# Scaling the other LoRA factor, and LoRA products by pairs of batches, in a fused two-layer conditional residual kernel

## The chip, the cores and the metric

One core of a Trainium2 chip. The metric is the device time of one execution in microseconds, lower is better. Median of three runs of the kernel before: 57.18 us (57.12 to 57.25).

## The reference

The input x is 8 batches x 512 tokens x 256 channels in float32, cond is 8 x 8. Two conditional linear layers follow each other, each with a residual:

```
w_bot = einsum('bg,got->bot', cond, weight * mask)            # weight 8 x 256 x 256
x = x + einsum('bnt,bot->bno', x, w_bot) + bias0
lora  = einsum('bter,eor,be->bto', einsum('btc,erc->bter', x, As), Bs, cond)   # As 8 x 16 x 256, Bs 8 x 256 x 16
x = x + einsum('btc,oc->bto', x, W_base) + b_base + 2 * lora
```

The 8 experts and 16 ranks of the second layer are together 128, one partition each.

## The kernel before

The kernel never computes the middle x. For each batch b it builds W0[b] = I + the mixed first weight, and W1[b] = I + base + LoRA, multiplies them to one 256 x 256 matrix M[b] (a merge), and applies M[b] to the tokens (an apply). Every matmul operand of merge, apply and LoRA is split into a high part, rounded to the reduced float32 format of TensorE, and a low part, the rest; `product` (lines 118 to 131) issues hi x hi, hi x lo and lo x hi, so each product is three matmuls per 128-row piece. In `product`, `mid_ready` is a wait before the second kind and `lo_ready` one before the third.

All engines run programs written out by hand in a fixed order and meet at semaphores.

- PE: 28 warm-up matmuls, lora(0), lora(1), then `mixed(0)` to `mixed(7)` (the first layer's weights, 128 columns each) with lora(2) and lora(3) among them; the first halves of merge 0 and 1; lora(4); the second halves of merge 0 and 1; apply(0); the two bias matmuls (line 547); then for b = 1 to 7: merge(b+1), apply(b), lora(b+4), as long as these exist (lines 550 to 555). A merge is 12 matmuls of 256 columns, an apply 12 of 512, a LoRA product 6 of 256: for each half j, A (scaled by batch b's condition) is the loaded operand and B the streamed one.
- ACT rounds the high parts: first eight `a_hi` (A_er times the condition of batch b), then W1_hi, W0_hi, x_hi, M_hi, and writes the output half 0 (`out0`), which adds bias_sb.
- DVE makes the low parts `a_lo`, x_lo and M_lo, adds base to each LoRA product (`w1`, line 323), masks the mixed weights (`w0`), does three dot products for the bias (line 362), puts bias_sb together (line 417) and writes the output half 1 (`out1`, line 357). Its loop at lines 422 to 427 runs out1(b-1), w1(b+3), x_lo(b+1), M_lo(b+1).
- POOL adds the identities and makes W0_lo and W1_lo.
- SP issues the loads and then the stores. ACT's queue issues the load of B (line 267) and of base.

PSUM has eight banks: ps_out0 to 3 (also used by mixed), ps_merge0 and 1, ps_lora0 and 1. LoRA product b goes to ps_lora[b % 2], both halves in one bank of 512 columns. The bias sums lie in ps_lora1; for that reason lora(4)'s w1 must be early, `pe.wait_ge(w1_done, 4)` stands before the bias matmuls, and lora(5) waits for bias_done. W1 has four buffers.

Of the kernel before, what the change touches and what calls it, by code (L numbers as in the profile page):

```python
# [5 lines left out]
def conditional_residual_kernel(nc: bass.Bass, head: bass.AP, rest: bass.AP, packs: bass.AP, factors_A: bass.AP,  # L6
# [22 lines left out]
    EXPW = KQ * C  # L29
    PACKW = EXPW + NT * TQ  # L30
    SCALING = 32.0 / 16
    LEAD = 4
    XBUF = 4
    W1BUF = 4
    WARM = 28
# [5 lines left out]
    with ExitStack() as ctx:  # L41
        def sb(name, shape, dt=f32):
            return ctx.enter_context(nc.sbuf_tensor(name, shape, dt))
# [4 lines left out]
        def sem(name):  # L48
            return ctx.enter_context(nc.semaphore(name))
# [28 lines left out]
        bias_sum = sb("bias_sum", [P, NT])  # L78
        base_bias0 = sb("base_bias0", [P, NT])
        low_bias = sb("low_bias", [P, NB])  # L80
        bias_sb = sb("bias_sb", [P, NT, NB])
        B_hi = sb("B_hi", [P, C], f32r)
        B_lo = sb("B_lo", [P, C], f32r)
        A_hi = sb("A_hi", [P, NB, C], f32r)
        A_lo = sb("A_lo", [P, NB, C], f32r)
# [18 lines left out]
        ps_out = [pb(f"ps_out{i}", [P, TOK]) for i in range(2 * NT)]  # L104
# [2 lines left out]
        ps_mix = ps_out  # L107
        ps_last = ps_lora[0][:, 0, :]

        ps_bias = ps_lora[1][:, 0, 0:NT * NB].rearrange("p (j b) -> p j b", j=NT)  # L110

# [5 lines left out]

        warm_set, ident_zero, ident_done = sem("warm_set"), sem("ident_zero"), sem("ident_done")  # L120
        base_done, dots_done, low_done, fixed_done = sem("base_done"), sem("dots_done"), sem("low_done"), sem("fixed_done")
        bias_mm, bias_done, bhi_done, blo_done = sem("bias_mm"), sem("bias_done"), sem("bhi_done"), sem("blo_done")

        ahi_done, alo_done = sem("ahi_done"), sem("alo_done")
        lora_mm, w1_done, w1hi_done, w1lo_done = sem("lora_mm"), sem("w1_done"), sem("w1hi_done"), sem("w1lo_done")
# [97 lines left out]

        @block.scalar
        def _(act):
            def a_hi(b):
                nc.scalar.activation(A_hi[:, b], A_er, ACT.Copy,
                                     scale=cond_er[:, b:b + 1]).then_inc(ahi_done, 1)

            def w1_hi(b):  # L230
                act.wait_ge(w1_done, b + 1)

                if b >= W1BUF:
                    act.wait_ge(merge_mm, b - W1BUF + 1)
                nc.scalar.activation(W1_hi[:, b % W1BUF], W1[:, b % W1BUF], ACT.Copy).then_inc(w1hi_done, 1)  # L235
# [34 lines left out]
            nc.scalar.activation(table_sb[:, :], warm[:, 0:1], ACT.Copy)  # L270
            act.dma_start(base_sb[:, :, :], base.rearrange("p (j o) -> p j o", j=NT)).then_inc(base_in, 16)

            act.wait_ge(lora_arrived, 16)
            for b in range(NB):
                a_hi(b)
            w1_hi(0)
            w1_hi(1)

# [23 lines left out]
            b = NB - 1  # L302
# [6 lines left out]
        def _(dve):  # L309
            nc.vector.memset(warm[:, :], 0.0).then_inc(warm_set, 1)  # L310

            def a_lo(b):
                dve.wait_ge(ahi_done, b + 1)
                nc.vector.scalar_tensor_tensor(out=A_lo[:, b], in0=A_er, scalar=cond_er[:, b:b + 1],
                                               in1=A_hi[:, b].bitcast(f32),
                                               op0=ALU.mult, op1=ALU.subtract).then_inc(alo_done, 1)

            def w1(b):
                dve.wait_ge(lora_mm, b + 1)
                if b >= W1BUF:  # L320

                    dve.wait_ge(w1lo_done, b - W1BUF + 1)
                nc.vector.tensor_tensor(W1[:, b % W1BUF], ps_lora[b % 2][:, :, :], base_sb[:, :, :],  # L323
                                        ALU.add).then_inc(w1_done, 1)

            def w0(q):
                dve.wait_ge(mix_mm, q + 1)
# [37 lines left out]
            def ramp_low(b):  # L365
                dve.wait_ge(ramp_hi, b + 2)
                nc.vector.tensor_tensor(W0_lo[:, b, :, H:C], W0[:, b, :, H:C], W0_hi[:, b, :, H:C].bitcast(f32),
                                        ALU.subtract).then_inc(ramp_lo, 1)

            dve.wait_ge(B_arrived, 16)  # L370
            nc.vector.tensor_scalar(B_hi[:, :], B_er, SCALING, None, ALU.mult).then_inc(bhi_done, 1)
            dve.wait_ge(bhi_done, 1)
            nc.vector.scalar_tensor_tensor(out=B_lo[:, :], in0=B_er, scalar=SCALING, in1=B_hi[:, :].bitcast(f32),
                                           op0=ALU.mult, op1=ALU.subtract).then_inc(blo_done, 1)
            dve.wait_ge(lora_arrived, 16)
            for b in range(NB):
                a_lo(b)
            nc.vector.tensor_tensor(bias_sum[:, :], bias0, bias1, ALU.add).then_inc(fixed_done, 1)
            dve.wait_ge(fixed_done, 1)
            w0(0)  # L380
# [26 lines left out]
            m_lo(1)  # L407
            split_x_lo(1)

            for j in range(NT):  # L410
                dve.wait_ge(dots_done, 1 + j)
                dot(base_rows[:, j, :], base_bias0[:, j:j + 1]).then_inc(dots_done, 1)
            dve.wait_ge(dots_done, 1 + NT)

            dve.wait_ge(bias_mm, 1)
            for j in range(NT):
                last = nc.vector.tensor_scalar(bias_sb[:, j, :], ps_bias[:, j, :], base_bias0[:, j:j + 1],
                                               bias_sum[:, j:j + 1], ALU.add, ALU.add)
            last.then_inc(bias_done, 1)
            dve.wait_ge(bias_done, 1)  # L420
            for b in range(1, NB):
                out1(b - 1)
                if b + 3 < NB:
                    w1(b + 3)
                if b + 1 < NB:
                    split_x_lo(b + 1)
                    m_lo(b + 1)
# [8 lines left out]
        def _(pe):  # L436
            def product(out, terms, lo_ready=None, mid_ready=None):


                for n, (hi_l, _, hi_r, _) in enumerate(terms):  # L440
                    nc.tensor.matmul(out, hi_l, hi_r, start=(n == 0), stop=False)  # L441
                if mid_ready is not None:
                    pe.wait_ge(*mid_ready)
                for hi_l, _, _, lo_r in terms:
                    nc.tensor.matmul(out, hi_l, lo_r, start=False, stop=False)  # L445
                if lo_ready is not None:
                    pe.wait_ge(*lo_ready)
                for n, (_, lo_l, hi_r, _) in enumerate(terms):
                    mm = nc.tensor.matmul(out, lo_l, hi_r, start=False, stop=(n == len(terms) - 1))  # L449
                return mm  # L450

            def lora(b):

                pe.wait_ge(ahi_done, b + 1)
                if b == 0:
                    pe.wait_ge(bhi_done, 1)
                if b >= 2:
                    pe.wait_ge(w1_done, b - 1)
                if b == 5:
                    pe.wait_ge(bias_done, 1)  # L460
                for j in range(NT):
                    cols = slice(j * P, (j + 1) * P)
                    mm = product(ps_lora[b % 2][:, j, :],
                                 [(A_hi[:, b, cols], A_lo[:, b, cols], B_hi[:, :], B_lo[:, :])],
                                 lo_ready=(alo_done, b + 1),
                                 mid_ready=(blo_done, 1) if b == 0 and j == 0 else None)
                mm.then_inc(lora_mm, 1)

            def mixed(q):
# [63 lines left out]
            for b in range(2):  # L533
                pe.wait_ge(ramp_hi, 1)
                pe.wait_ge(w1lo_done, b + 1)
                merge_half(b, 0, (ramp_first, 1))
            lora(4)
            for b in range(2):
                pe.wait_ge(ramp_hi, 2 + b)
                merge_half(b, 1, (ramp_lo, 1 + b)).then_inc(merge_mm, 1)  # L540

            pe.wait_ge(w0_done, NQ)
            apply(0)
            pe.wait_ge(w1_done, 4)
# [5 lines left out]
            for b in range(1, NB):  # L550
                if b + 1 < NB:
                    merge(b + 1)
                apply(b)
                if b + LEAD < NB:
                    lora(b + LEAD)


# [52 lines left out]
```

## Time and profile before

| | |
|---|---|
| median of 3 runs | 57.18 us (57.12 to 57.25) |
| profiled execution, its own time | 57.23 us |
| its span in the trace | 55.4 us, 997 instructions |
| PE busy | 51.7 us, 93% of the span |
| DVE busy | 42.1 us, 76% |
| ACT busy | 31.5 us, 57% |
| POOL busy | 31.2 us, 56% |
| DMA | 11.79 MB, mean 213 GB/s |

Times are microseconds from the start of the span. PE is the matmul stream; matmuls are pipelined, so the distance from one start to the next is the pace, and the printed duration of a matmul is longer than that. The duration of a row with x2 or more is from the first start to the last end of the group. The number in brackets is the idle time of the engine before the row and what ended it. 1.8 us lie outside the span and inside the measured time.

### The profile page before, as it was taken

The numbers are of one execution on the slowest core, as the hardware profiler recorded it, in microseconds if no ns is written. First come the engines' busy times: TensorE is split into PE (matmuls) and PEld (weight loads), VectorE is DVE, ScalarE is ACT, GpSimd is POOL, SyncE is SP. The second block draws the span as 40 slices with busy tenths as digits, with TensorE's granted clock in tenths as the row PEclk, the third lists the DMA queues.
The fourth block names the chain that finished last, engine by engine and source line by source line (L and its number), as shares of the span: only waits on it lengthen the run. The fifth ranks groups of instructions, "written<-read, shape, count | busy, mean of one in ns | idle before, by whom it ended". The sixth has DMA issues, their size and how long they took to land.

```text
span 55.4 us, 997 instructions
## 1 busy us (share of the span) xinstructions
PE 51.7 (93%) x342; PEld 47.1 (85%) x342; DVE 42.1 (76%) x64; ACT 31.5 (57%) x52; POOL 31.2 (56%) x30
## 2 busy tenths in 40 slices
PE   2999999999999999999999999999999999999900
PEld 2988999999999888988998898899889889888800
DVE  0039999979596998999999999979929959805030
ACT  1949900447807889440999925970993950840800
POOL 4003400299980099999909999999966990000000
PEclk9999999999999999999999999999999999999999
DMA  0699999999999994000082540090054045049572
GB/s 0 133 392 335 373 366 389 419 418 425 408 396 417 417 393 169 9 0 0 0 306 78 222 169 0 15 364 0 6 195 183 0 185 194 0 179 382 197 284 95
DMA packets 5476, 11.79 MB, mean 213 GB/s; under 512 B 608, under 2 KB 1376, under 8 KB 5472
## 3 DMA queue, kind: packets, MB, share of 16 engines
q1 hardware_dynamic: 5184, 11.35, 54.6%
q10 hardware_dynamic: 288, 0.39, 1.9%
q8 instruction: 2, 0.03, 0.3%
q14 instruction: 2, 0.02, 0.1%
HBM read 7.54 MB, written 4.19 MB: 212 GB/s over the span
## 4 chain that ended last, share of the span: by engine, by line
PE 93%; DVE 1%; issue 0%
PE ps_out L441 13%; PE ps_out L483 13%; PE ps_out L445 13%; PE ps_out L449 13%; PE ps_merge L441 7%; PE ps_merge L445 7%; PE ps_merge L449 7%; PE ps_merge L522 6%; PE ps_lora L441 5%; PE ps_lora L445 5%; PE ps_lora L449 5%; DVE out_sb L432 1%; PE ps_lora L547 1%; DVE warm L310 0%
## 5 line engine op out<-in xcount | busy, mean ns | idle before, releaser
L189 POOL TENSOR_TENSOR W_lo<-W,W_hi 128x512 fp32r<-128x512 f32 x8 | 10.5, 1314 | 7.1 <-ACT W_hi L235 7.1
L342 DVE TENSOR_TENSOR x_lo<-x_sb,x_hi 128x1024 fp32r<-128x1024 f32 x8 | 12.7, 1584 | 0.0
L195 POOL TENSOR_TENSOR W_lo<-W,W_hi 128x512 fp32r<-128x512 f32 x6 | 10.9, 1824 | 0.0
L441 PE MATMUL ps_out<-x_hi,M_hi 128*128 128x512 f32 (+1 forms) x32 | 9.8, 388 | 0.0
L445 PE MATMUL ps_out<-x_lo,M_hi 128*128 128x512 f32 (+1 forms) x32 | 9.7, 384 | 0.0
L449 PE MATMUL ps_out<-x_hi,M_lo 128*128 128x512 f32 (+1 forms) x32 | 9.7, 384 | 0.0
L248 ACT ACTIVATE M_hi<-ps_merge 128x512 fp32r<-128x512 f32 x8 | 4.8, 597 | 8.0 <-PE ps_merge L449 8.0
L255 ACT ACTIVATE x_hi<-x_sb 128x1024 fp32r<-128x1024 f32 x8 | 8.4, 1053 | 0.0
L199 POOL TENSOR_TENSOR W<-W,ident 128x256 f32<-128x256 f32 x6 | 6.6, 1099 | 3.0 <-DVE x_lo L342 3.0
L357 DVE TENSOR_SCALAR out_sb<-ps_out,bias_sb 128x512 f32<-128x512 f32 x7 | 5.2, 747 | 3.5 <-PE ps_out L449 3.4
L264 ACT ACTIVATE out_sb<-ps_out,bias_sb 128x512 f32<-128x512 f32 x8 | 5.5, 685 | 3.9 <-PE ps_out L449 2.2
L483 PE MATMUL ps_out<-packs_sb 128*128 128x128 f32 x64 | 7.6, 275 | 0.0
L483 PEld LDWEIGHTS ps_out<-packs_sb 128*128 128x128 f32 x64 | 7.4, 192 | 0.0
L235 ACT ACTIVATE W_hi<-W 128x512 fp32r<-128x512 f32 x8 | 5.0, 626 | 3.9 <-DVE W L323 3.8
L449 PEld LDWEIGHTS ps_out<-x_hi,M_lo 128*128 128x128 f32 x32 | 5.9, 188 | 1.2
L445 PEld LDWEIGHTS ps_out<-x_lo,M_hi 128*128 128x128 f32 x32 | 5.9, 188 | 1.2
L441 PE MATMUL ps_merge<-W_hi 128*128 128x256 f32 x32 | 6.7, 291 | 0.0
L445 PE MATMUL ps_merge<-W_lo,W_hi 128*128 128x256 f32 x32 | 6.4, 283 | 0.0
L449 PE MATMUL ps_merge<-W_hi,W_lo 128*128 128x256 f32 x32 | 6.4, 282 | 0.0
L441 PEld LDWEIGHTS ps_out<-x_hi,M_hi 128*128 128x128 f32 x32 | 5.5, 189 | 0.9 <-issue 0.2
L331 DVE TENSOR_TENSOR W<-ps_out,packs_sb 128x512 f32<-128x512 f32 x8 | 5.4, 686 | 0.9 <-PE ps_out L483 0.9
L349 DVE TENSOR_TENSOR M_lo<-ps_merge,M_hi 128x512 fp32r<-128x512 f32 x8 | 5.5, 682 | 0.4 <-ACT M_hi L248 0.4
(50 smaller groups left out, 80.1 us busy)
## 6 DMA issues: line engine op xcount, KB each, us to landing
x_sb<-xT_dram SPq DMA_DIRECT2D x8, 512.0 KB, 10.2
outT_dram<-out_sb SPq DMA_DIRECT2D x15, 256.0 KB, 2.3
packs_sb<-packs_dram SPq DMA_DIRECT2D x7, 288.0 KB, 5.3
rows_sb<-rows_dram SPq DMA_DIRECT2D x1, 384.0 KB, 6.8
base_sb<-base_dram ACTq DMA_DIRECT2D x1, 256.0 KB, 3.6
outT_dram<-out_sb SPq DMA_DIRECT2D x2, 128.0 KB, 1.8
packs_sb<-head_dram SPq DMA_DIRECT2D x1, 192.0 KB, 3.4
packs_sb<-rest_dram SPq DMA_DIRECT2D x1, 160.0 KB, 3.6
```

The source lines that it names most:

```text
L189: pool.tensor_tensor(W1_lo[:, b % W1BUF], W1[:, b % W1BUF], W1_hi[:, b % W1BUF].bitcast(f32), ALU.subtract).then_inc(w1lo_done, 1)
L195: pool.tensor_tensor(W0_lo[:, b % 2], W0[:, b], W0_hi[:, b % 2].bitcast(f32), ALU.subtract).then_inc(w0lo_done, 1)
L199: pool.tensor_tensor(diagonal(b), diagonal(b), ident[:, :].unsqueeze(1).to_broadcast([P, NT, P]), ALU.add).then_inc(eye_done, 1)
L255: nc.scalar.activation(x_hi[:, b % XBUF], x_sb[:, b], ACT.Copy).then_inc(xhi_done, 1)
L264: nc.scalar.activation(out_sb[:, b % 2, 0, :], ps_out[b % 2 * NT][:, :], ACT.Identity, bias=bias_sb[:, 0, b:b + 1]).then_inc(out_done[0], 1)
L331: nc.vector.tensor_tensor(W0[:, :, :, ts].rearrange("p b j t -> p j b t"), ps_mix[q % 4][:, :].rearrange("p (j b t) -> p j b t", j=NT, t=T ...
L342: nc.vector.tensor_tensor(x_lo[:, b % XBUF], x_sb[:, b], x_hi[:, b % XBUF].bitcast(f32), ALU.subtract).then_inc(xlo_done, 1)
L349: nc.vector.tensor_tensor(M_lo[:, b % 2], ps_merge[b % 2][:, :, :], M_hi[:, b % 2].bitcast(f32), ALU.subtract).then_inc(mlo_done, 1)
L441: nc.tensor.matmul(out, hi_l, hi_r, start=(n == 0), stop=False)
L445: nc.tensor.matmul(out, hi_l, lo_r, start=False, stop=False)
L449: mm = nc.tensor.matmul(out, lo_l, hi_r, start=False, stop=(n == len(terms) - 1))
L483: mm = nc.tensor.matmul(dst[:, j, :, k, :], pack(q)[0][:, k, j * P:(j + 1) * P], mix, start=True, stop=True)
```

## The change

Three things change.

1. The condition of batch b now scales B, not A. `a_hi(b)` and `a_lo(b)` become `b_hi(b)` on ACT and `b_lo(b)` on DVE, eight each as before; the factor 2 is now on A, split once on DVE. ACT waits for both loads before its first b_hi. A is the same for all batches, so two batches can be streamed behind one loaded operand.
2. LoRA products 4 to 7 go by pairs: `lora_pair(4)` takes the place of lora(4), `lora_pair(6)` comes after apply(2), and no LoRA product follows apply(1) and apply(3). A pair is 6 matmuls of 512 columns (two batches of 256); half j goes to ps_lora[j]. DVE's `w1_pair` adds base in two operations of 512 columns, one per half, at b = 1 and b = 3 of its loop, where the single w1(4) to w1(7) ran at b = 1 to 4.
3. The bias sums move to ps_out3. DVE reads them with one operation (`low_sum`, adding bias_sum) before the two base dots, and PE waits for that read before the second half of apply(1). bias_sb is then one operation instead of two.

```diff
-        ps_bias = ps_lora[1][:, 0, 0:NT * NB].rearrange("p (j b) -> p j b", j=NT)
+        ps_bias = ps_out[3][:, 0:NT * NB].rearrange("p (j b) -> p j b", j=NT)
...
-            def a_hi(b):
-                nc.scalar.activation(A_hi[:, b], A_er, ACT.Copy,
-                                     scale=cond_er[:, b:b + 1]).then_inc(ahi_done, 1)
+            def b_hi(b):
+                nc.scalar.activation(B_hi[:, b], B_er, ACT.Copy,
+                                     scale=cond_er[:, b:b + 1]).then_inc(bhi_done, 1)
             def w1_hi(b):
-                act.wait_ge(w1_done, b + 1)
+                act.wait_ge(w1_done, b + 1 if b < SINGLE else b // 2 * 2 + 2)
...
+            act.wait_ge(B_arrived, 16)
             act.wait_ge(lora_arrived, 16)
             for b in range(NB):
-                a_hi(b)
+                b_hi(b)
...
+            def w1_pair(b):
+                dve.wait_ge(lora_mm, SINGLE + (b - SINGLE) // 2 + 1)
+                dve.wait_ge(w1lo_done, b - W1BUF + 2)
+                at = b % W1BUF
+                for j in range(NT):
+                    nc.vector.tensor_tensor(W1[:, at:at + 2, j, :], ps_lora[j][:, :, :],
+                                            base_sb[:, j, :].unsqueeze(1).to_broadcast([P, 2, C]),
+                                            ALU.add).then_inc(w1_done, 1)
...
+            dve.wait_ge(lora_arrived, 16)
+            nc.vector.tensor_scalar(A_hi[:, :], A_er, SCALING, None, ALU.mult).then_inc(ahi_done, 1)
+            dve.wait_ge(ahi_done, 1)
+            nc.vector.scalar_tensor_tensor(out=A_lo[:, :], in0=A_er, scalar=SCALING, in1=A_hi[:, :].bitcast(f32),
+                                           op0=ALU.mult, op1=ALU.subtract).then_inc(alo_done, 1)
             dve.wait_ge(B_arrived, 16)
...
+            dve.wait_ge(bias_mm, 1)
+            nc.vector.tensor_tensor(low_sum[:, :, :], ps_bias, bias_sum[:, :].unsqueeze(2).to_broadcast([P, NT, NB]),
+                                    ALU.add).then_inc(bias_read, 1)
             for j in range(NT):
                 dve.wait_ge(dots_done, 1 + j)
                 dot(base_rows[:, j, :], base_bias0[:, j:j + 1]).then_inc(dots_done, 1)
             dve.wait_ge(dots_done, 1 + NT)
-            dve.wait_ge(bias_mm, 1)
-            for j in range(NT):
-                last = nc.vector.tensor_scalar(bias_sb[:, j, :], ps_bias[:, j, :], base_bias0[:, j:j + 1],
-                                               bias_sum[:, j:j + 1], ALU.add, ALU.add)
-            last.then_inc(bias_done, 1)
+            dve.wait_ge(bias_read, 1)
+            nc.vector.tensor_tensor(bias_sb[:, :, :], low_sum[:, :, :],
+                                    base_bias0[:, :].unsqueeze(2).to_broadcast([P, NT, NB]), ALU.add).then_inc(bias_done, 1)
             dve.wait_ge(bias_done, 1)
             for b in range(1, NB):
                 out1(b - 1)
-                if b + 3 < NB:
-                    w1(b + 3)
+                if b == 1 or b == 3:
+                    w1_pair(b + 3)
...
             def lora(b):
-                if b == 5:
-                    pe.wait_ge(bias_done, 1)
...
                     mm = product(ps_lora[b % 2][:, j, :],
-                                 [(A_hi[:, b, cols], A_lo[:, b, cols], B_hi[:, :], B_lo[:, :])],
-                                 lo_ready=(alo_done, b + 1),
-                                 mid_ready=(blo_done, 1) if b == 0 and j == 0 else None)
+                                 [(A_hi[:, cols], A_lo[:, cols], B_hi[:, b], B_lo[:, b])],
+                                 lo_ready=(alo_done, 1) if b == 0 and j == 0 else None,
+                                 mid_ready=(blo_done, b + 1) if j == 0 else None)
...
+            def lora_pair(b):
+                pe.wait_ge(blo_done, b + 2)
+                pe.wait_ge(w1_done, b)
+                both = slice(b, b + 2)
+                for j in range(NT):
+                    cols = slice(j * P, (j + 1) * P)
+                    mm = product(ps_lora[j][:, :, :], [(A_hi[:, cols], A_lo[:, cols], B_hi[:, both], B_lo[:, both])])
+                mm.then_inc(lora_mm, 1)
...
+                    if b == 1 and i == 1:
+                        pe.wait_ge(bias_read, 1)
...
-            lora(4)
+            lora_pair(4)
...
-            pe.wait_ge(w1_done, 4)
             pe.wait_ge(low_done, 1)
...
                 apply(b)
-                if b + LEAD < NB:
-                    lora(b + LEAD)
+                if b == 2:
+                    lora_pair(6)
```

## Rows read from the trace of the kernel before

**Rows 1.** Chain of work that ended last, share of the span by engine.
```profile
PE 93%; DVE 1%; issue 0%
```

**Rows 2.** PE in order of time, 26 to 30 us: start, duration, engine, line, operation.
```profile
26.65 0.28 PE L441 MATMUL ps_lora<-B_hi,A_hi 128*128 128x256 f32 x1
...
27.37 0.40 PE L441 MATMUL ps_merge<-W_hi 128*128 128x256 f32 x2
...
28.81 0.63 PE L441 MATMUL ps_out<-x_hi,M_hi 128*128 128x512 f32 x2
29.27 0.62 PE L445 MATMUL ps_out<-x_lo,M_hi 128*128 128x512 f32 x2
29.74 0.62 PE L449 MATMUL ps_out<-x_hi,M_lo 128*128 128x512 f32 x2
```

**Rows 3.** All engines in order of time, 3 to 6 us.
```profile
3.50 3.30 ACT L227 ACTIVATE A_hi<-lora_sb 128x256 fp32r<-128x256 f32 x8 [0.82 <-DMA lora_sb<-factors_A_dram]
3.68 0.29 DVE L371 TENSOR_SCALAR B_hi<-lora_sb 128x256 fp32r<-128x256 f32 x1 [2.75 <-DMA lora_sb<-factors_B_dram]
...
4.35 3.66 DVE L314 SCALAR_TENSOR_TENSOR A_lo<-lora_sb,A_hi 128x256 fp32r<-128x256 f32 x8
...
4.49 0.58 PE L445 MATMUL ps_lora<-B_lo,A_hi 128*128 128x256 f32 x1
...
5.26 0.41 PE L441 MATMUL ps_lora<-B_hi,A_hi 128*128 128x256 f32 x1
...
5.47 0.41 PE L445 MATMUL ps_lora<-B_lo,A_hi 128*128 128x256 f32 x1
```

**Rows 4.** PE in order of time: behind lora(4), and the bias matmuls.
```profile
17.46 0.50 PE L441 MATMUL ps_merge<-W_hi 128*128 128x256 f32 x2
...
22.03 0.51 PE L547 MATMUL ps_lora<-low_bias,lora_sb 128*128 128x8 f32 x4
```

**Rows 5.** DVE in order of time, from 19 us on.
```profile
19.86 0.66 DVE L362 CUSTOM_DVE_ANT_0 row_products<-lora_sb,rows_sb 128x256 f32<-128x256 f32 x1
...
21.42 0.69 DVE L349 TENSOR_TENSOR M_lo<-ps_merge,M_hi 128x512 fp32r<-128x512 f32 x1 [0.27 <-ACT M_hi L248]
22.02 1.43 DVE L342 TENSOR_TENSOR x_lo<-x_sb,x_hi 128x1024 fp32r<-128x1024 f32 x1
23.38 0.97 DVE L362 CUSTOM_DVE_ANT_0 row_products<-rows_sb 128x256 f32<-128x256 f32 x1
...
24.39 1.39 DVE L362 CUSTOM_DVE_ANT_0 row_products<-rows_sb 128x256 f32<-128x256 f32 x1
...
25.82 0.48 DVE L417 TENSOR_SCALAR bias_sb<-ps_lora,base_bias,bias_sum 128x8 f32<-128x8 f32 x2
...
27.00 0.68 DVE L323 TENSOR_TENSOR W<-ps_lora,base_sb 128x512 f32<-128x512 f32 x1
27.60 1.22 DVE L342 TENSOR_TENSOR x_lo<-x_sb,x_hi 128x1024 fp32r<-128x1024 f32 x1
28.73 0.68 DVE L349 TENSOR_TENSOR M_lo<-ps_merge,M_hi 128x512 fp32r<-128x512 f32 x1
...
30.59 2.19 DVE L342 TENSOR_TENSOR x_lo<-x_sb,x_hi 128x1024 fp32r<-128x1024 f32 x1
...
41.55 0.75 DVE L357 TENSOR_SCALAR out_sb<-ps_out,bias_sb 128x512 f32<-128x512 f32 x1 [0.99 <-PE ps_out L449]
```

**Rows 6.** ACT in order of time, 18 to 21 us.
```profile
18.48 0.60 ACT L248 ACTIVATE M_hi<-ps_merge 128x512 fp32r<-128x512 f32 x1 [0.24 <-PE ps_merge L449]
...
20.27 0.63 ACT L241 ACTIVATE W_hi<-W 128x512 fp32r<-128x512 f32 x1 [0.24 <-POOL W L199]
20.80 0.58 ACT L248 ACTIVATE M_hi<-ps_merge 128x512 fp32r<-128x512 f32 x1
```

**Rows 7.** POOL in order of time, beside the dots and x_lo(3).
```profile
24.02 1.47 POOL L189 TENSOR_TENSOR W_lo<-W,W_hi 128x512 fp32r<-128x512 f32 x1
...
30.40 1.30 POOL L195 TENSOR_TENSOR W_lo<-W,W_hi 128x512 fp32r<-128x512 f32 x1
```

More of the change, by code:

```diff
@@ L31, in conditional_residual_kernel @@
     SCALING = 32.0 / 16
-    LEAD = 4
+    SINGLE = 4
     XBUF = 4
@@ L80, in conditional_residual_kernel @@
         low_bias = sb("low_bias", [P, NB])
+        low_sum = sb("low_sum", [P, NT, NB])
         bias_sb = sb("bias_sb", [P, NT, NB])
[L82 to L85, printed above, removed]
+        A_hi = sb("A_hi", [P, C], f32r)
+        A_lo = sb("A_lo", [P, C], f32r)
+        B_hi = sb("B_hi", [P, NB, C], f32r)
+        B_lo = sb("B_lo", [P, NB, C], f32r)
         W1 = sb("W1", [P, W1BUF, NT, C])
@@ L121, in conditional_residual_kernel @@
         base_done, dots_done, low_done, fixed_done = sem("base_done"), sem("dots_done"), sem("low_done"), sem("fixed_done")
-        bias_mm, bias_done, bhi_done, blo_done = sem("bias_mm"), sem("bias_done"), sem("bhi_done"), sem("blo_done")
+        bias_mm, bias_read, bias_done, bhi_done, blo_done = sem("bias_mm"), sem("bias_read"), sem("bias_done"), sem("bhi_done"), sem("blo_done")
         ahi_done, alo_done = sem("ahi_done"), sem("alo_done")
@@ L310, in _, with b_lo @@
             nc.vector.memset(warm[:, :], 0.0).then_inc(warm_set, 1)
[L312 to L316, printed above, removed]
+            def b_lo(b):
+                dve.wait_ge(bhi_done, b + 1)
+                nc.vector.scalar_tensor_tensor(out=B_lo[:, b], in0=B_er, scalar=cond_er[:, b:b + 1],
+                                               in1=B_hi[:, b].bitcast(f32),
+                                               op0=ALU.mult, op1=ALU.subtract).then_inc(blo_done, 1)
             def w1(b):
                 dve.wait_ge(lora_mm, b + 1)
-                if b >= W1BUF:
-                    dve.wait_ge(w1lo_done, b - W1BUF + 1)
-                nc.vector.tensor_tensor(W1[:, b % W1BUF], ps_lora[b % 2][:, :, :], base_sb[:, :, :],
+                nc.vector.tensor_tensor(W1[:, b], ps_lora[b % 2][:, :, :], base_sb[:, :, :],
                                         ALU.add).then_inc(w1_done, 1)
+            def w1_pair(b):
[6 more added lines that the diff above has]
+                                            ALU.add).then_inc(w1_done, 1)
             def w0(q):
@@ L368, in ramp_low @@
                                         ALU.subtract).then_inc(ramp_lo, 1)
-            dve.wait_ge(B_arrived, 16)
[L371 to L375, printed above, removed]
+            dve.wait_ge(lora_arrived, 16)
[3 more added lines that the diff above has]
+                                           op0=ALU.mult, op1=ALU.subtract).then_inc(alo_done, 1)
+            dve.wait_ge(B_arrived, 16)
             for b in range(NB):
-                a_lo(b)
+                b_lo(b)
             nc.vector.tensor_tensor(bias_sum[:, :], bias0, bias1, ALU.add).then_inc(fixed_done, 1)
@@ L452, in lora @@
             def lora(b):
-                pe.wait_ge(ahi_done, b + 1)
+                pe.wait_ge(bhi_done, b + 1)
                 if b == 0:
-                    pe.wait_ge(bhi_done, 1)
+                    pe.wait_ge(ahi_done, 1)
                 if b >= 2:
                     pe.wait_ge(w1_done, b - 1)
-                if b == 5:
-                    pe.wait_ge(bias_done, 1)
                 for j in range(NT):
```

## Prediction

> **What bounds the kernel now.** I read the shares of the chain of work that ended last first: PE has 93% of it, DVE 1%, and issue nothing [rows 1]. So nearly every microsecond of the span is a matmul behind a matmul, and an edit counts only if it changes what PE streams or makes PE wait. The order of PE's matmuls in time then gives the pace. Six LoRA matmuls of 256 columns go from 26.65 to 27.37, 0.12 us each; twelve merge matmuls of 256 columns from 27.37 to 28.81, again 0.12 each; in the apply the first four of 512 columns go from 28.81 to 29.74, 0.2325 each [rows 2]. Next I looked at the start, where PE meets its first operands [rows 3], at the one matmul pair in the middle that is longer than its kind [rows 4], and last at DVE in order of time from 19 us on. After M_lo(1) at 21.42 each of DVE's operations down to x_lo(3) at 30.59 begins as the one before it ends: x_lo(1), the bias dots, bias_sb, out1(0), w1(4), then batch 2's operands [rows 5]. It is not on the chain, but there it is the engine that is nearly late.
>
> **How nearly.** apply(2) needs x_lo(2) for its third matmul at 29.27 and M_lo(2) for its fifth at 29.74. DVE ends x_lo(2) at 27.60 + 1.22 = 28.82 and M_lo(2) at 28.73 + 0.68 = 29.41 [rows 2, 5]. With about 0.05 for the signal (the wait at 21.42 is told by ACT's M_hi(1), 20.80 + 0.58 = 21.38, rows 5 and 6) the slack is 0.40 and 0.28 us. That is what the change spends.
>
> **The change on PE.** *Columns.* The four single products of batches 4 to 7 are 24 matmuls of 256 columns, 24 x 0.12 = 2.88 us. The two pairs are 12 of 512, 12 x 0.2325 = 2.79. Gain 0.09. Below, the gain could be nothing, above 0.15. The number of columns is the same; only the fixed part per matmul is halved in count: 2 x 0.12 - 0.2325 = 0.0075 us each.
>
> The Trainium skill (TensorE: Matmul & The Clock Gate, Back-to-back issue gap) puts the warm gap at columns over 2.4 GHz plus 2.5 ns; by that the twelve saved issues are worth 0.03 us instead of 0.09. The trace's 0.12 for 256 columns is above that rule's 0.109, so the rows decide.
>
> *Where the pair stands.* lora_pair(4) takes the place of lora(4) between the first and the second halves of merges 0 and 1. It is 6 x 0.2325 = 1.40 instead of 0.72, so what comes after it is 0.68 later. The first pair of matmuls behind it shows 0.50 [rows 4] where its like shows 0.40 [27.37, rows 2]: 0.10 us in which PE waits for W0_hi. With 0.68 more cover that wait goes: gain 0.10 (0 if it isn't a wait). After apply(1) no LoRA product follows any more, 0.72 less; after apply(2) the second pair stands, 0.68 more; after apply(3) none, 0.72 less. lora_pair(4) also needs w1(3) out of its bank. On DVE w1(3) stands ahead of w0(7), and that ahead of the W0_hi for which PE waited only these 0.10 us, one product later; I cost that wait at nothing.
>
> *Start.* ACT now waits for B besides A. A's wake is ACT's 3.50, B's is DVE's 3.68 [rows 3], so b_hi(0) starts 0.2 later, about 3.70. The first b_lo follows it as a_lo follows at 4.35 at the earliest: b_hi(0) ends near 4.20, b_lo(0) runs 4.24 to 4.72. DVE's two A operations take the place of its two B operations and start 0.18 earlier, so they are out of the way. PE's second matmul, now waiting for b_lo(0), goes from 4.49 to about 4.77; but its third no longer waits for a_lo(0), since A_lo is long done. So the fourth, at 5.26 before, comes at 4.77 + 0.16 for a load that wasn't ahead + 2 x 0.21 (pace 5.26 to 5.47, which is 256 columns at 1.2 GHz) = 5.35. Cost 0.09, of which about half is at the half clock and so is regained when the clock rises at the same moment: I take 0.08, with 0 and 0.20 as ends. After that ACT and DVE run ahead of PE as before. No DMA is added, taken away or moved on any queue.
>
> **The bias move.** The two bias matmuls keep their number and place. On DVE low_sum is added right behind x_lo(1), and the two bias_sb operations (0.48 for two, rows 5) become one: +0.24 and -0.24. low_sum waits for bias_mm: PE's bias matmuls go from 22.03 [rows 4] to 22.7 and are done near 23.2, DVE is there at 23.8; hidden. PE's new wait for bias_read stands before apply(1)'s second half, at about 25.9 when low_sum is done by 24.1; hidden by 1.8 us, and if it weren't, merge(3) and apply(2) would queue behind it. Between nothing and 0.3 on DVE; I take 0.
>
> **The DVE side, which sets the sum.** (1) M_hi(0) on ACT starts at 18.48 + 0.68 + 0.08 - 0.10 = 19.14. From it to M_hi(1) ACT took 20.80 - 18.48 = 2.32, with 0.24 of idle that a later start absorbs [rows 6], so 2.0 to 2.1: M_hi(1) at 21.19, done 21.77. M_lo(1) moves from 21.42 to 21.80, +0.37, and with it everything DVE does without a gap behind it. (2) w1_pair(4) is two operations where w1(4) was one; from 27.00 to 27.60 [rows 5] one costs 0.60. The second stands before x_lo(2): +0.60. Together 0.97: x_lo(2) ends at 29.79, M_lo(2) at 30.38. In exchange w1(5) is gone one round later, which is too late to help. On ACT W1_hi(4) now waits for both halves of the pair, from 28.6; behind it are M_hi(3) and out0(1), which nothing on PE needs before apply(3).
>
> PE wants M_lo(2) at 29.74 + 0.68 + 0.08 - 0.10 - 0.72 = 29.68, since LoRA(5) no longer stands between apply(1) and merge(3). It gets it at 30.38 + 0.05 = 30.43: a stall of 0.75, in two parts, since x_lo(2) is already late by 29.84 - 29.21 = 0.63 at the third matmul. They don't add; the later one sets it. The removed LoRA(5) was, without being meant so, part of DVE's cover.
>
> **After that.** lora_pair(6) stands behind apply(2), 1.40 us of PE work that needs no DVE operation in time, so DVE catches up: with out1(1) before it, x_lo(3) ends at latest at 31.1 + 2.19 = 33.3, while apply(3) reaches it at 30.43 + 8 x 0.2325 + 1.40 + 1.44 + 0.47 = 35.6. Before apply(4) DVE has w1_pair(6), +0.60 again, but from there on it waits for PE (0.99 idle at 41.55, rows 5). I cost it at nothing; if that cover were gone it would be at most 0.60. The end, ps_last and the stores aren't touched.
>
> **Sum.** -0.09 - 0.10 + 0.08 + 0.75 = +0.64. The profiled execution took 57.23, the median is 57.18, 0.05 lower: 57.82, so about 57.8. The likeliest case's own range is 57.5 to 58.1.
>
> **Rivals.** *A, no stall, from the dots (faster or same).* DVE's two base dots take 0.97 and 1.39 us from 23.38 and 24.39, the bias dot of the same form 0.66 [rows 5]. The second meets POOL's w1_lo(3), 24.02 to 25.49 [rows 7]. If the later start lets both dots pass when POOL is idle, DVE regains up to 0.31 + 0.73 = 1.04 us, more than the 0.97 it lost. The mechanism decides at 0.75 regained; then what is left is -0.11 (-0.24 with the better ends of columns and start): 56.95 to 57.1. Against it: POOL's work is paced by the same ACT and is busy almost throughout this stretch, so it moves with the dots.
>
> *B, more collision (slower yet).* x_lo(2) takes 1.22 because POOL is idle then; x_lo(3), started at 30.59 within POOL's operation at 30.40, takes 2.19 [rows 5, 7]. Later by a microsecond, x_lo(2) or a dot may land in one: +0.3 to +1.0, 58.1 to 58.8. For it: low_sum shifts the dots against POOL. Against: POOL's w1_lo(4) waits for ACT's W1_hi(4), which itself waits for w1_pair(4).
>
> The Trainium skill (GPSIMD Engine Reference, Specifications) says that GpSimd's SBUF interfaces are shared with VectorE and that an operation with two SBUF inputs contends. The 1.22 against 2.19 agrees.
>
> *C, the start.* The longer gap before the second matmul could also keep the clock at 1.2 GHz for longer; each microsecond of it costs half. The pace is still 0.21 at 5.47 and 0.12 in the middle [rows 2, 3]; with 1 us more of it, +0.5: 58.3.
>
> *D, the change doesn't gain columns at all:* +0.09 on the forecast, inside its range.
>
> **Chances.** Forecast (with D) 0.60; A 0.20, of which 0.13 faster and 0.07 within 0.2%; B 0.13; C 0.07. About 0.2% (0.11 us) is what a measurement here tells from no change. Faster 0.13, same 0.07, slower 0.80. The range leaves out most of faster A and the far end of B: 57.1 to 58.4.
>
> **What would show it.** After: PE idle of 0.6 to 0.9 before the third and fifth matmul of apply(2), put down to DVE x_lo and M_lo; DVE without idle from 21.8 to there; the pair behind lora_pair(4) at 0.40 instead of 0.50; 512-column LoRA matmuls 0.23 apart; first mixed matmul 0.05 to 0.10 later. It is wrong if apply(2) runs without a gap (A), if the base dots or x_lo(2) change their durations by over 0.3 (A or B), or if the pace of 0.21 lasts longer than in the kernel before (C).

## The result: slower by 2.8%, where 1.1% was forecast

| | before | changed |
|---|---|---|
| median of 6 runs | 57.3 us (57.12 to 57.63) | 59.7 us (58.94 to 61.01) |
| ratio | | 1.0284, 95% interval 1.0235 to 1.0334 |
| profiled execution, its own time | 57.23 us | 58.97 us |
| its span | 55.4 us | 57.2 us |
| PE busy | 51.7 us | 51.3 us |
| DVE busy | 42.1 us | 44.4 us |

The ratio compares undisturbed runs; three of the six of the changed kernel, at 60.4 to 61.0, were disturbed and only raise its median. The difference to explain is that of the two profiled executions: 58.97 - 57.23 = +1.74 us. The forecast was 57.8, range 57.1 to 58.4. The sign and the place were right, the size was not.

The chain of work that ended last, changed kernel, shares of the span. Before it was PE with 93% [rows 1]:

```profile
PE 66%; DVE 19%; DMA 5%; issue 4%; ACT 1%; DVEq 0%
```

PE in order of time, changed kernel: start, duration, engine, line, operation, idle before and what ended it. `product`'s three kinds are L449, L453, L457 here:

```profile
16.65 0.40 PE L449 MATMUL ps_lora<-B_hi,A_hi 128*128 128x512 f32 x1
...
18.04 0.40 PE L449 MATMUL ps_merge<-W_hi 128*128 128x256 f32 x2
...
22.47 0.60 PE L564 MATMUL ps_out<-low_bias,lora_sb 128*128 128x8 f32 x4
22.93 0.48 PE L449 MATMUL ps_merge<-W_hi 128*128 128x256 f32 x2
...
28.62 0.67 PE L449 MATMUL ps_out<-x_hi,M_hi 128*128 128x512 f32 x2
30.83 0.73 PE L453 MATMUL ps_out<-x_lo,M_hi 128*128 128x512 f32 x2 [1.54 <-DVE x_lo L350]
31.43 0.73 PE L457 MATMUL ps_out<-x_hi,M_lo 128*128 128x512 f32 x2
32.00 0.63 PE L449 MATMUL ps_out<-x_hi,M_hi 128*128 128x512 f32 x2
```

apply(2) begins at 28.62, 0.19 us earlier than before [28.81, rows 2]. At the pace of before its fifth matmul would stand at 28.62 + 0.93 = 29.55. It stands at 31.43: a stall of 1.88 us. The next pair follows 0.57 later instead of 0.46, so the stop costs 1.99 in all. The rest, -0.25, is the gain at other places. The first pair of matmuls behind lora_pair(4) shows 0.40, not 0.50 [rows 4]; lora_pair(4) took 18.04 - 16.65 = 1.39. From the first bias matmul to the merge behind it are 22.93 - 22.47 = 0.46 us, 0.36 before (22.03 to 22.39): low_bias ended only at 22.41, and where it is early (the experiment with the first dot moved) the distance is 0.36 again.

DVE in order of time, changed kernel, the lines that answer to [rows 5]. `row_products` is a dot, L370 with `lora_sb` the first one, with `rows_sb` alone the two base dots:

```profile
20.19 0.92 DVE L370 CUSTOM_DVE_ANT_0 row_products<-lora_sb,rows_sb 128x256 f32<-128x256 f32 x1
...
21.16 1.25 DVE L412 TENSOR_SCALAR low_bias<-lora_sb,A_bias 128x8 f32<-128x8 f32 x1
22.33 0.68 DVE L357 TENSOR_TENSOR M_lo<-ps_merge,M_hi 128x512 fp32r<-128x512 f32 x1
22.93 1.23 DVE L350 TENSOR_TENSOR x_lo<-x_sb,x_hi 128x1024 fp32r<-128x1024 f32 x1
24.08 0.16 DVE L419 TENSOR_TENSOR low_sum<-ps_out,bias_sum 128x16 f32<-128x16 f32 x1
24.17 1.43 DVE L370 CUSTOM_DVE_ANT_0 row_products<-rows_sb 128x256 f32<-128x256 f32 x1
...
25.64 1.39 DVE L370 CUSTOM_DVE_ANT_0 row_products<-rows_sb 128x256 f32<-128x256 f32 x1
...
27.07 0.59 DVE L426 TENSOR_TENSOR bias_sb<-low_sum,base_bias 128x16 f32<-128x16 f32 x1
27.70 0.75 DVE L365 TENSOR_SCALAR out_sb<-ps_out,bias_sb 128x512 f32<-128x512 f32 x1
28.36 1.28 DVE L330 TENSOR_TENSOR W<-ps_lora,base_sb 128x512 f32<-128x512 f32 x2
29.56 1.22 DVE L350 TENSOR_TENSOR x_lo<-x_sb,x_hi 128x1024 fp32r<-128x1024 f32 x1
30.69 0.68 DVE L357 TENSOR_TENSOR M_lo<-ps_merge,M_hi 128x512 fp32r<-128x512 f32 x1
```

POOL and ACT beside them, changed kernel:

```profile
19.39 1.44 POOL L200 TENSOR_TENSOR W<-W,ident 128x256 f32<-128x256 f32 x2 [2.93 <-DVE x_lo L350]
...
20.92 0.59 ACT L249 ACTIVATE M_hi<-ps_merge 128x512 fp32r<-128x512 f32 x1
21.10 1.29 POOL L196 TENSOR_TENSOR W_lo<-W,W_hi 128x512 fp32r<-128x512 f32 x1 [0.26 <-ACT W_hi L242]
...
23.04 2.27 POOL L190 TENSOR_TENSOR W_lo<-W,W_hi 128x512 fp32r<-128x512 f32 x1
25.28 1.47 POOL L196 TENSOR_TENSOR W_lo<-W,W_hi 128x512 fp32r<-128x512 f32 x1
26.71 0.92 POOL L200 TENSOR_TENSOR W<-W,ident 128x256 f32<-128x256 f32 x1
```

POOL and low_bias in the kernel before:

```profile
19.49 1.63 POOL L199 TENSOR_TENSOR W<-W,ident 128x256 f32<-128x256 f32 x2 [3.02 <-DVE x_lo L342]
20.56 0.59 DVE L404 TENSOR_SCALAR low_bias<-lora_sb,A_bias 128x8 f32<-128x8 f32 x1
```

x_lo(2) starts at 29.56 instead of 27.60: DVE is 1.96 us later, where 0.97 was forecast. Read the two engines side by side. low_bias works on 8 columns and takes 1.25 us, from 21.16 to 22.41, because POOL's W0_lo(2) runs from 21.10 to 22.39. Its 0.59 before was a wait too, only a shorter one: it ended at 21.15, POOL's second identity add at 21.12. The first dot came up during POOL's first identity add before (the first of the x2, over at 20.23), and in the changed kernel, 0.33 later, during the second (over at 20.83); both times it ended 0.28 behind that add. ACT's M_hi(1) stands at 20.92, only 0.12 later than before [rows 6], so it isn't ACT that holds M_lo(1) back, it is DVE's own row of operations.

The slip, step by step: M_lo(1) starts 22.33 - 21.42 = 0.91 later (0.37 forecast); from there to bias_sb it is 4.74 instead of 4.40, +0.34; from bias_sb to out1(0) and on to x_lo(2), with the second half of w1_pair, 2.49 instead of 1.78, +0.71. Sum 1.96.

### The profile page after: what moved, and what is told of

It is laid out like the page before. It is cut to its first block, busy times and chain, and to the rows that moved or that the text cites. A ratio compares the mean times of both kernels' runs of the same rounds, so it can differ in the third digit from the quotient of the medians.

```text
span 57.2 us, 969 instructions
## 1 busy us (share of the span) xinstructions
PE 51.3 (90%) x330; PEld 45.4 (80%) x330; DVE 44.4 (78%) x64; ACT 31.3 (55%) x52; POOL 31.2 (55%) x30
## 4 chain that ended last, share of the span: by engine, by line
PE 66%; DVE 19%; DMA 5%; issue 4%; ACT 1%; DVEq 0%
PE ps_out L499 12%; PE ps_out L453 10%; PE ps_out L457 9%; PE ps_out L449 8%; DMA lora_sb<-factors_A_dram 5%; PE ps_merge L457 5%; PE ps_merge L453 5%; PE ps_merge L449 5%; PE ps_lora L453 4%; DVE x_lo L350 4%; PE ps_lora L449 4%; DVE row_products L370 4%; PE ps_lora L457 4%; DVE M_lo L357 2%; DVE W L330 2%
## 5 line engine op out<-in xcount | busy, mean ns | idle before, releaser
L350 DVE TENSOR_TENSOR x_lo<-x_sb,x_hi 128x1024 fp32r<-128x1024 f32 x8 | 13.4, 1676 | 0.0
L453 PE MATMUL ps_out<-x_lo,M_hi 128*128 128x512 f32 (+1 forms) x32 | 9.8, 387 | 1.5 <-DVE x_lo L350 1.5
L449 PE MATMUL ps_out<-x_hi,M_hi 128*128 128x512 f32 (+1 forms) x32 | 9.9, 389 | 0.0
L457 PE MATMUL ps_out<-x_hi,M_lo 128*128 128x512 f32 (+1 forms) x32 | 9.8, 387 | 0.0
L453 PEld LDWEIGHTS ps_out<-x_lo,M_hi 128*128 128x128 f32 x32 | 5.9, 188 | 3.1 <-DVE x_lo L350 2.0
L457 PEld LDWEIGHTS ps_out<-x_hi,M_lo 128*128 128x128 f32 x32 | 5.9, 188 | 1.5 <-DVE M_lo L357 0.3
L449 PE MATMUL ps_merge<-W_hi 128*128 128x256 f32 x32 | 6.6, 287 | 0.0
L457 PE MATMUL ps_merge<-W_hi,W_lo 128*128 128x256 f32 x32 | 6.4, 283 | 0.0
L453 PE MATMUL ps_merge<-W_lo,W_hi 128*128 128x256 f32 x32 | 6.4, 283 | 0.0
L449 PEld LDWEIGHTS ps_out<-x_hi,M_hi 128*128 128x128 f32 x32 | 5.5, 189 | 0.9 <-issue 0.2
```

Of the source, the lines that this page charges most:

```text
L350: nc.vector.tensor_tensor(x_lo[:, b % XBUF], x_sb[:, b], x_hi[:, b % XBUF].bitcast(f32), ALU.subtract).then_inc(xlo_done, 1)
```

## The experiments

Ratios are to the kernel before, with their 95% interval. The changed kernel stands at 1.0284 and 58.97 us. Edits are shown against the changed kernel. Theory 1: the loss is DVE being late for apply(2), through the pair's place. Its rivals: the start (2), the bias move (3), the 512 columns themselves (4). Theory 5, formed on the first results: DVE's operations with SBUF operands wait for POOL's running operation, and this doubles the slip.

One distance is free of an early or late start and of the stores at the end: from the first merge matmul to the last group of matmuls, both read in order of time. It is 52.27 - 15.23 = 37.04 us before and 54.01 - 15.13 = 38.88 in the changed kernel. Below it is called the stream.

### The first part of the change alone

```diff
-            lora_pair(4)
+            lora(4)
...
-                if b == 1 or b == 3:
-                    w1_pair(b + 3)
+                if b + 3 < NB:
+                    w1(b + 3)
```

Bias sums and their code are those of before as well.

> The kernel before with only the first part of the change: the condition scales B; LoRA products all single, bias sums in the LoRA bank as before. Theory 1 (the loss comes from DVE being late for apply(2), by the pair's work and by collisions with POOL that the pair's delay brings): no change, 57.1 to 57.4, ratio 0.997 to 1.003, and no gap in apply(2). Rival 2 (the start costs): 57.5 or more with the first mixed matmul later than 6.74.

Measured: 57.42 median, fastest 57.12, ratio 1.0015 (0.9975 to 1.0055). Scaling B instead of A costs nothing that can be measured, and by the interval at most 0.3 us. The profiled execution itself, 57.80 us, has its first mixed matmul at 7.03, 0.29 later than before, which alone would look like rival 2. But with the same scaling it stands at 6.28 in the changed kernel and at 6.19 two experiments below, and the stream here is 37.02. The start differs from one execution to the next; rival 2 is out as the cause of 2.8%.

### The scaling and the bias move, products single

The same two edits for the pairs, and the bias sums as in the changed kernel.

> The scaling of B and the move of the bias sums, LoRA products all single. Theory 1: within 0.2 of the kernel before, 57.1 to 57.5; low_bias near 0.6 us, since M_lo(0) isn't delayed. Rival 3 (the bias move, with low_sum and its waits, makes the loss): 58 or more, and PE waits in apply(1) or apply(2).

Measured: 58.11 median, fastest 57.74, ratio 1.0152 (1.0098 to 1.0206). I had this wrong: with the bias move the kernel is 1.5% slower, and the scaling alone showed none of it. DVE in this kernel:

```profile
20.54 0.58 DVE L414 TENSOR_SCALAR low_bias<-lora_sb,A_bias 128x8 f32<-128x8 f32 x1
...
25.78 1.14 DVE L428 TENSOR_TENSOR bias_sb<-low_sum,base_bias 128x16 f32<-128x16 f32 x1
...
28.22 1.22 DVE L352 TENSOR_TENSOR x_lo<-x_sb,x_hi 128x1024 fp32r<-128x1024 f32 x1
```

and POOL:

```profile
25.42 1.47 POOL L196 TENSOR_TENSOR W_lo<-W,W_hi 128x512 fp32r<-128x512 f32 x1
```

bias_sb adds 16 columns from SBUF to SBUF and takes 1.14 us. It ends at 26.92, POOL's W0_lo(3) at 26.89. The two operations it replaces read PSUM and took 0.48 together [rows 5]. x_lo(2) starts 0.62 later than before, and PE waits for it in apply(2). The stream is 37.55, so this stop is 0.51 of the loss; the profiled executions differ by 58.00 - 57.23 = 0.77, and the other 0.26 lies outside the stream and stays open. The next experiment asks whether it is bias_sb, or low_sum and PE's wait for it.

### The same with bias_sb made by ACT

```diff
...
-            nc.vector.tensor_tensor(bias_sb[:, :, :], low_sum[:, :, :],
-                                    base_bias0[:, :].unsqueeze(2).to_broadcast([P, NT, NB]), ALU.add).then_inc(bias_done, 1)
...
+                    for j in range(NT):
+                        act.wait_ge(dots_done, 2 + j)
+                        nc.scalar.activation(bias_sb[:, j, :], low_sum[:, j, :], ACT.Identity,
+                                             bias=base_bias0[:, j:j + 1]).then_inc(bias_done, 1)
```

> The scaling of B and the bias move with single products, and bias_sb made by ACT (two small operations from low_sum) instead of DVE's one operation of 1.14 us. Theory 5 (an operation of DVE that reads two SBUF operands waits until POOL's running operation is over, here W0_lo(3), and that alone made the bias move cost 0.5 us or more): x_lo(2) starts at 27.6 instead of 28.22, no gap in apply(2), 57.1 to 57.4, ratio below 1.005. Rival (low_sum, the bank or PE's wait for it cost it): stays at 57.8 to 58.1.

Measured: 57.52 median, fastest 57.13, ratio 0.9996 (0.9957 to 1.0035). The whole 1.5% is gone. DVE:

```profile
26.00 0.75 DVE L372 TENSOR_SCALAR out_sb<-ps_out,bias_sb 128x512 f32<-128x512 f32 x1 [0.43 <-DVE base_bias L377]
...
27.27 1.23 DVE L357 TENSOR_TENSOR x_lo<-x_sb,x_hi 128x1024 fp32r<-128x1024 f32 x1
```

The forecast said 27.6, it is 27.27 (0.17 of the difference to 28.22 is an earlier start), apply(2) has no gap, and the stream is 37.02. The bank, low_sum (0.16, reads PSUM) and PE's wait are still there; only the operation that met POOL isn't.

### Products of 256 columns at the pairs' place

```diff
-                    mm = product(ps_lora[j][:, :, :], [(A_hi[:, cols], A_lo[:, cols], B_hi[:, both], B_lo[:, both])])
+                    for k in range(2):
+                        mm = product(ps_lora[j][:, k, :], [(A_hi[:, cols], A_lo[:, cols], B_hi[:, b + k], B_lo[:, b + k])])
```

> The changed kernel with each product of 512 columns as two of 256, at the same place and in the same banks. Theory 1: the place makes the loss and 512 columns are worth only 0.07 us for each pair, so 59.0 to 59.2 against 58.97 for the changed kernel, still a gap of 1.7 to 2.0 in apply(2). Rival 4 (512-column products are themselves slow, or hold a bank longer): 57.3 to 58.

Measured: 60.38 median, fastest 60.19, ratio 1.0572 (1.0516 to 1.0628). The trace has the stall where it was, the time is 1.2 us above what I expected:

```profile
28.88 0.66 PE L449 MATMUL ps_out<-x_hi,M_hi 128*128 128x512 f32 x2
31.07 0.73 PE L453 MATMUL ps_out<-x_lo,M_hi 128*128 128x512 f32 x2 [1.53 <-DVE x_lo L350]
```

From 28.88 to 31.07 are 2.19 us, 2.21 in the changed kernel; rival 4 is out. The stream is 39.02, 0.14 more than in the changed kernel: about what the 512 columns are worth. At the end ACT's last whole output waits for an earlier store:

```profile
54.41 0.69 ACT L265 ACTIVATE out_sb<-ps_out,bias_sb 128x512 f32<-128x512 f32 x1 [3.11 <-DMA outT_dram<-out_sb]
```

The changed kernel has 2.03 of idle time there, put down to PE. So by this one profile about 1 us of its time is a late store. Why all six of its runs are above 60 stays open, since one profile shows one store.

### w1_pair(4) after x_lo(2) and M_lo(2)

```diff
-                if b == 1 or b == 3:
+                if b == 3:
                     w1_pair(b + 3)
                 if b + 1 < NB:
                     split_x_lo(b + 1)
                     m_lo(b + 1)
+                if b == 1:
+                    w1_pair(b + 3)
```

> The changed kernel with one move: on DVE w1_pair(4) comes after x_lo(2) and M_lo(2) instead of before them. Theory 1: both are 1.2 us earlier, the stall in apply(2) falls from 1.88 to 0.7, the time to 57.8; up to 58.4 if merge(4) then waits for W1_lo(4), which follows w1_pair(4) over ACT and POOL. Rival (DVE's late start into x_lo(2) isn't what ends the wait): 58.9 as before.

Measured: 59.58 median, fastest 59.51, ratio 1.042 (1.038 to 1.0461), slower than the changed kernel. PE:

```profile
28.89 0.65 PE L451 MATMUL ps_out<-x_hi,M_hi 128*128 128x512 f32 x2
29.89 0.74 PE L455 MATMUL ps_out<-x_lo,M_hi 128*128 128x512 f32 x2 [0.34 <-DVE x_lo L350]
30.49 0.73 PE L459 MATMUL ps_out<-x_hi,M_lo 128*128 128x512 f32 x2
...
34.67 0.48 PE L451 MATMUL ps_merge<-W_hi 128*128 128x256 f32 x2 [0.71 <-issue]
...
35.87 0.50 PE L459 MATMUL ps_merge<-W_hi,W_lo 128*128 128x256 f32 x2 [0.49 <-POOL W_lo L196]
```

The stall in apply(2) is 30.49 - 28.89 - 0.93 = 0.67, as expected. But merge(4) then waits twice, 0.71 and 0.49 of idle PE. Read from start to start it is more: from the last LoRA matmul, 33.57, to apply(3), 36.92, are 3.35 us, and 36.17 - 34.51 = 1.66 in the changed kernel, so merge(4) loses 1.69 where apply(2) had won 1.21. The stream is 39.52. POOL shows why:

```profile
32.37 2.19 POOL L190 TENSOR_TENSOR W_lo<-W,W_hi 128x512 fp32r<-128x512 f32 x1 [4.49 <-ACT W_hi L236]
34.52 1.30 POOL L196 TENSOR_TENSOR W_lo<-W,W_hi 128x512 fp32r<-128x512 f32 x1
```

W1_lo(4) meets x_lo(3) on DVE (32.20 to 33.41) and takes 2.19 instead of 1.3, and W0_lo(4) comes behind it. My bound for this, 58.4, left that collision out. The wait moved from one place to the next.

### The first dot into a time when POOL is idle

```diff
+            dve.wait_ge(rows_in, 16)
+            dot(A_er, A_bias0[:, :]).then_inc(dots_done, 1)
             ramp_low(0)
...
-            dve.wait_ge(rows_in, 16)
-            dot(A_er, A_bias0[:, :]).then_inc(dots_done, 1)
```

> The changed kernel with the first bias dot (A times bias0) moved ahead of W0_lo's second halves on DVE, into a gap of 0.48 us, to a time when POOL is idle. Theory 5: the dot takes 0.66 instead of 0.92, low_bias comes sooner, M_lo(1) starts at 21.55 instead of 22.33, DVE is 0.5 to 0.8 us earlier at x_lo(2), the stall in apply(2) falls from 1.88 to 1.1 to 1.4, time 58.2 to 58.5. Rival (the dots' place doesn't matter, they are absorbed later): 58.95.

Measured: 58.29 median, fastest 58.17, ratio 1.0182 (1.0122 to 1.0241), 0.7 us less than the changed kernel. DVE:

```profile
16.78 0.42 DVE L370 CUSTOM_DVE_ANT_0 row_products<-lora_sb,rows_sb 128x256 f32<-128x256 f32 x1
...
20.19 0.66 DVE L412 TENSOR_SCALAR low_bias<-lora_sb,A_bias 128x8 f32<-128x8 f32 x1
21.53 0.69 DVE L357 TENSOR_TENSOR M_lo<-ps_merge,M_hi 128x512 fp32r<-128x512 f32 x1 [0.68 <-ACT M_hi L249]
```

The dot takes 0.42 with POOL idle, 0.66 before, 0.92 in the changed kernel. low_bias takes 0.66 instead of 1.25; it still waits for POOL, whose second identity add ends at 20.82, low_bias at 20.85. M_lo(1) is back to waiting for ACT, at 21.53 as expected, and the stall in apply(2) is 1.30. Of the 0.80 us that M_lo(1) gained x_lo(2) keeps 0.70: the first base dot is down to 0.88 from 1.43, but bias_sb, earlier now, meets another POOL operation and takes 1.14 instead of 0.59.

### Without the base dots

The two dots and their share of the bias are left out; bias_sb stays, with bias_sum in the place of what the dots gave.

> The changed kernel without the two base dots (the term base times bias0 is left out of the bias): DVE has 2.9 us less to do before x_lo(2). Theory 1: no stall in apply(2) at all, 57.0 to 57.2, which is the changed kernel's 58.97 less the stall of 1.88; so everything but the stall is a small gain against the kernel before. Rival 3 (start or pairs cost by themselves): 57.5 or more.

Measured: 56.95 median, fastest 56.84, ratio 0.9946 (0.9908 to 0.9983). apply(2) runs through:

```profile
28.55 0.63 PE L445 MATMUL ps_out<-x_hi,M_hi 128*128 128x512 f32 x2
29.02 0.62 PE L449 MATMUL ps_out<-x_lo,M_hi 128*128 128x512 f32 x2
29.48 0.62 PE L453 MATMUL ps_out<-x_hi,M_lo 128*128 128x512 f32 x2
```

So with DVE out of the way the rest of the change is worth about 0.3 us, 0.5%. The stream is 36.89, 0.15 less than before; the rest is an earlier start, which the runs don't tie to the change. That is about the most that the pairs can bring at these places.

### Filling the hole that LoRA(5) left

```diff
+                if b == 3:
+                    merge_half(b, 0, (w0lo_done, b - 1))
                 for i in range(NT):
```

> The changed kernel with 6 more matmuls of 256 columns, 0.72 us, in merge(3): its first half is computed twice, with the same result. They stand where LoRA(5) stood before. Theory 1: PE waits for DVE anyway, so nothing changes: 58.9 to 59.1, the stall in apply(2) 1.16 instead of 1.88. Rival (PE's own stream sets the end): 59.6 to 59.7.

Measured: 59.98 median, fastest 59.21, ratio 1.0349 (1.028 to 1.0418). Its times spread too much to settle it (59.21 to 60.61). In the profiled execution everything from the mixed matmuls on is 1.46 us later (first merge matmul 16.59, changed kernel 15.13), so I compare distances from there:

```profile
16.59 0.48 PE L449 MATMUL ps_merge<-W_hi 128*128 128x256 f32 x2
...
30.81 0.63 PE L449 MATMUL ps_out<-x_hi,M_hi 128*128 128x512 f32 x2
32.29 0.73 PE L453 MATMUL ps_out<-x_lo,M_hi 128*128 128x512 f32 x2 [0.84 <-DVE x_lo L350]
32.89 0.74 PE L457 MATMUL ps_out<-x_hi,M_lo 128*128 128x512 f32 x2
```

The third matmul of apply(2) stands 32.29 - 16.59 = 15.70 behind the first merge matmul, and 30.83 - 15.13 = 15.70 in the changed kernel. The stall is 1.15 instead of 1.88. 0.72 us of added PE work vanished in the wait, and the stream is 38.92, against 38.88.

### Two versions with DVE relieved

Both make the first dot early and bias_sb on ACT. The first also reorders:

```diff
             for b in range(1, NB):
-                out1(b - 1)
+                if b > 1:
+                    out1(b - 1)
...
                     m_lo(b + 1)
+                if b == 1:
+                    dve.wait_ge(bias_done, 2)
+                    out1(0)
```

> The changed kernel with DVE relieved and reordered: the first dot ahead of W0_lo's second halves, bias_sb made by ACT, and between the base dots and batch 3 the order w1_pair(4), x_lo(2), M_lo(2), out1(0). Theories 1 and 5: DVE ends the dots at 25.8, w1_pair at 27.0, x_lo(2) at 28.2, M_lo(2) at 28.8, before apply(2) needs them at 28.98 and 29.44, and out1(0) at 29.4, before its bank is needed at 29.9. No gap: 56.9 to 57.1, ratio 0.993 to 0.998. Rival (pairs on their own cost what they gain): 57.2 or more.

Measured: 57.26 median, fastest 56.95, ratio 0.9998 (0.9955 to 1.004). The profiled execution is again one with a late start (first merge matmul 16.68):

```profile
30.82 1.40 DVE L370 TENSOR_SCALAR out_sb<-ps_out,bias_sb 128x512 f32<-128x512 f32 x2
...
31.01 0.68 PE L462 MATMUL ps_out<-x_hi,M_lo 128*128 128x512 f32 x2
31.61 0.73 PE L454 MATMUL ps_out<-x_hi,M_hi 128*128 128x512 f32 x2
32.18 0.62 PE L458 MATMUL ps_out<-x_lo,M_hi 128*128 128x512 f32 x2
```

Of the stall some 0.25 us is left (0.60 and 0.57 between starts where 0.46 is the pace). It is no longer x_lo or M_lo: the second half of apply(2) waits for out1(0), the first of the two operations at 30.82, to free its bank. The stream is 37.07, 37.04 before. The loss of 2.8% is gone; a gain over the kernel before isn't measurable.

> As the reordered kernel, but w1_pair(4) stands after M_lo(2), out1(0) before x_lo(2), and POOL makes W0_lo(4) before W1_lo(4). Theory 1: no gap in apply(2), since M_lo(2) ends at 28.8; but W1_lo(4) then comes at 31.9 to 33, and merge(4) wants it at 32.7: 57.0 to 57.4. Rival (the late pair's chain over ACT and POOL is longer than that, as in the kernel with the late pair alone): 57.5 to 58.5.

Measured: 57.28 median, fastest 57.14, ratio 0.9985 (0.9948 to 1.0023). merge(4) waits 0.22 for W1_lo(4), no other gap; the stream is 37.24. So no version here beats the kernel before beyond the measurement.

## Why the prediction was wrong

**Bounds and place: right.** DVE's order into apply(2) was the thing to watch, and the slack of 0.28 us before it was right: 1.96 of slip, 0.28 of slack and PE's 0.19 earlier arrival give 1.96 - 0.28 + 0.19 = 1.87, measured 1.88.

**The step that failed** is (1) of the DVE side: "M_lo(1) moves from 21.42 to 21.80, +0.37, and with it everything DVE does without a gap behind it". It took M_lo(1) to follow ACT's M_hi(1), moved the operations and kept their durations. M_hi(1) came at 20.92, not 21.19, and would have let M_lo(1) start 0.11 later, at the 21.53 of the kernel with the early dot. What held it back was DVE itself: a chain shifted against POOL meets other operations of POOL. M_lo(1) moved 0.91: the first dot grew from 0.66 to 0.92 and low_bias from 0.59 (0.58 in the kernel with single products) to 1.25. The base dots grew by 0.46 in sum, x_lo(1) shrank by 0.20. Of the 0.99 us by which the slip exceeds the forecast, 0.54 lie before M_lo(1), 0.34 from there to bias_sb, and 0.11 behind. Moving the dot alone brought M_lo(1) to 21.53 and 0.7 us back, which shows the first part. The second is read from the traces: both base dots end 0.28 to 0.29 us behind a POOL operation in each of the eleven kernels that have them, but no run moves them to an idle POOL.

**The bias move, costed at nothing,** "between nothing and 0.3 on DVE", was mis-sized: -0.24 assumed that one operation costs half of two. It reads SBUF on both sides where the two read PSUM, and waits for POOL: 1.14 us in the kernel with single products, and the 1.5% went with it. In the changed kernel it happened to meet the last 0.56 us of POOL's identity add (26.71 to 27.63), and took 0.59. That it cost little there is luck.

**The second half of w1_pair** was +0.60, measured 0.59 (from out1(0) to x_lo(2) 1.86 instead of 1.27). **The lost cover of LoRA(5)** is confirmed by the filler. **Columns:** 0.09 forecast; lora_pair(4) took 1.39 where the same place with single products took 1.44, lora_pair(6) 1.36 instead of 1.43, together 0.12. **The wait behind lora(4)** went, 0.10. **Start:** costed at +0.08; lora(2) came at 10.14 in the changed kernel, 0.09 before the other's, and the scaling alone is 1.0015, so it is not measurable. About half of PE's 0.19 earlier arrival at apply(2) is this start, which was not forecast and varies from one execution to the next.

**The rivals.** B, more collision, was what happened, at a chance of 0.13 and a price of 0.3 to 1.0 us; it cost 0.99 of the 1.88 - 0.75 = 1.13 by which the stall was larger, and PE's earlier arrival the rest. It was named for x_lo(2) or one dot; what grew was the first dot, low_bias, the first base dot, and bias_sb against its price, while x_lo(2) kept its 1.22. One collision was priced where four followed each other, and the range's upper end of 58.4 cut even that one short. Its sign, a base dot changed by more than 0.3, was named and came: 0.97 to 1.43. A took the same mechanism in the other direction and bet on luck of 1.04 us; it took the 0.66 of the first dot for its price beside an idle POOL, but that was partly a wait too, and the idle price is 0.42. C did not come: starts 0.21 apart ended by 5.10 in the changed kernel and by 6.11 before, and only at 6.65 in the profile with the scaling alone, so this too is the execution's and not the edit's.

## What to carry to other kernels

When a chain on DVE shifts in time, its durations don't come along: lay POOL's operations beside it at the new times before adding up. A duration read from one trace may already be partly a wait; subtract POOL's end from the operation's end, and if the same small number comes each time, it is. A tiny operation that reads only SBUF can cost a whole POOL operation; let it read PSUM, give it to ACT, or put it where POOL is idle. And before PE work is moved or removed, ask which other engine it was giving time to.

## What the runs showed of the hardware

A DVE operation that reads only SBUF and came up while a POOL operation ran ended nearly the same time behind POOL's end, wherever the twelve traces have one of these: the dots 0.28 to 0.29 us (0.42 when POOL was idle), x_lo 1.08 to 1.19 (1.22 when POOL was idle), low_bias' 8 columns and bias_sb's 16 columns 0.03. So it waited for the whole rest of POOL's operation, and its duration tells when it came up, not how much it does: low_bias took from 0.58 to 1.33. No trace has low_bias or this bias_sb beside an idle POOL, so their own price isn't shown. Operations with an operand in PSUM did not wait: low_sum kept 0.16 and M_lo 0.67 to 0.69 in every kernel that has them, beside POOL or not. It works the other way too: where x_lo started first, POOL's W_lo took up to 2.3 us instead of 1.3, as W1_lo(3) here, 2.27 beside DVE's x_lo(1).

The Trainium skill (GPSIMD Engine Reference, Specifications) names a VectorE operation with two SBUF inputs, or one in a two-port mode, as the one that contends. The dots, x_lo and bias_sb are of the first kind, and the traces agree. low_bias has one tensor and pointer scalars and waited as well; no row shows the mode that it ran in, so that it is of the second kind isn't shown.
